# The patch transforms of a convolution block on 64 by 64 tiles of TensorE

## The chip, the cores and the metric

The program runs on one core of a Trainium2 chip. A core has a matrix engine (PE, or TensorE, whose weight loads are a row of their own, PEld), a vector engine (DVE), a scalar engine (ACT), GpSimd (POOL) and SyncE (SP), which here only issues DMAs. The engines run their own instruction streams and meet at semaphores. Matmuls write to PSUM, eight banks of 512 float32 columns on each of 128 partitions; SBUF holds everything else. The metric is the device time of the program in microseconds.

## The reference

Two blocks on an image batch x of 4 by 64 by 64 pixels with 16 channels, all in float32. The first mixes channels in the two-dimensional Fourier domain and ends with a depthwise convolution. The second, whose main loop is changed here, is

```
hidden = layernorm(x) @ w_hidden                     # 16 -> 192
q, k, v = split(conv3x3(hidden, w_qkv), 3)           # 64 channels each
out = irfft2(rfft2(patches(q)) * rfft2(patches(k)))  # 8 by 8 patches
out = v * layernorm(out)                             # over the 64 channels
return out @ w_out + x
```

The product of spectra is a circular convolution of q and k on each patch. A patch has 64 pixels. Its real spectrum is kept as 64 real numbers: 32 "first" ones (real parts) and 32 "second" ones (imaginary parts; the four purely real frequencies are paired up among them).

## The kernel before, in words

The second block runs as a loop of 16 steps `s`. A step handles 1024 pixels, two halves `n = 2s` and `2s + 1` of 512 pixels. What each engine does in a step is written out by hand in a loop over `s` in that engine's block, and the order in that loop is the order of its queue. The pieces, with the names used below (a function is named by what it is called in the code; its index `i` is the step whose data it works on):

- `gather(n)` on DVE and `gather9(n)` on ACT copy the convolution's input windows out of SBUF buffers (`ui`, `ui9`, both in `arena`) into `tile` and `tile9` (L394). `conv(n)` on PE (L1356) multiplies them with the folded weights into banks 0 and 1; `conv_out(n)` on ACT (L773) copies q, k and v of 512 pixels out, into one of four `qkv` buffers. The 64 pixels of a patch lie on 64 partitions, two patches on 128, so a transform contracts over 64 partitions.
- `forward(i)` on PE (L1369), one step later: k's spectrum into banks 4 and 5 (with constant `fk`), then q's into banks 2 and 3 (with `fq`). Each is two matmuls of a 64 by 128 weight tile with 512 columns. The 128 output rows are the spectrum twice over, for q as (first, second, first, second), for k as (first, second, second, first), so that one elementwise product holds all four products that a complex product needs.
- `k_out(i)` on ACT (L780) copies k's 1024 columns to `kh`; `product(i)` on DVE (L1008) multiplies q's 1024 columns in PSUM with it into `pr`.
- `inverse(i)` on PE (L1389): two matmuls of a 128 by 64 weight tile (`inv4`) with 512 columns, into bank 6.
- The layer norm: `o_sum` (L1017) and `o_centre` (L1023) on DVE read bank 6, `o_square` on ACT (L791), `o_variance` on DVE (L1037), `root` on ACT (L761), `o_scale` on DVE (L1042, L1043). In the loop these work on the data of step `s - 2`, whose inverse ended the step before.
- `gate` on POOL (L608 to L610), then `turn(s - 3)` on PE (L1409), four 128 by 128 transposes into bank 7, `turned` on ACT (L767), and for two of four steps `unit(u)` on PE (L1435), which projects 16 image columns, `unit_out` on ACT (L801) and `finish(u)` on DVE (L1055, L447), a transpose and the residual sum. `finish` stands at the end of DVE's steps 6, 7, 10, 11 and 14.

DVE's order in a step is `o_sum`, `o_centre`, `o_variance`, `gather(2s+1)`, `gather(2s+2)`, `o_scale`, `product`, then what is extra in that step. `forward(i)` and `product(i)` are guarded by one buffer each: `product(i)` waits for `inverse(i-1)`, `inverse(i)` for `o_centre(i-1)`.

The input of the second image pair (index `g` = 1, loop steps 8 to 15) is made during the loop. After `bordered(1)` (L889) has written it, `part` on ACT (L655, L658) and `split` on DVE (L882, L884) cut it in three bfloat16 parts; `split(1, 0)` makes two subtractions, one for each image, and `split(1, 1)` two more. SP stores the image (`store_padded`, L484) and its parts (`store_parts`, L490) to DRAM, and loads them back as convolution windows with `load_chunk(g, th, b2)`: three DMAs of `load_taps` (L499) and four of `load_last` (L506, L509), some 1.6 MB. `gather(16)` and `gather9(16)` in step 7 are the first that need a chunk of the second pair, `gather(20)` in step 9 the next.

## Time and profile before

| | us |
|---|---|
| median of 3 runs (220.47 to 221.62) | 220.53 |
| the profiled execution | 220.6 |
| its span, first to last instruction | 218.8 |
| PE busy | 205.2 (94%) |
| DVE busy | 158.2 (72%) |
| ACT busy | 131.7 (60%) |
| POOL busy | 78.2 (36%) |

The granted TensorE clock is 1.00 of full speed over the whole span. PE's busy share is high in every slice of the page except a few; the loop of 16 steps runs from about 89 us to the end.
### The profile page before, as it was taken

The numbers are of one execution on the slowest core, as the hardware profiler recorded it, in microseconds if no ns is written. First come the engines' busy times: TensorE is split into PE (matmuls) and PEld (weight loads), VectorE is DVE, ScalarE is ACT, GpSimd is POOL, SyncE is SP. The second block draws the span as 40 slices with busy tenths as digits, with TensorE's granted clock in tenths as the row PEclk, the third lists the DMA queues.
The fourth block names the chain that finished last, engine by engine and source line by source line (L and its number), as shares of the span: only waits on it lengthen the run. The fifth ranks groups of instructions, "written<-read, shape, count | busy, mean of one in ns | idle before, by whom it ended". The sixth has DMA issues, their size and how long they took to land.

```text
span 218.8 us, 4503 instructions
## 1 busy us (share of the span) xinstructions
PE 205.2 (94%) x1716; PEld 129.9 (59%) x1716; DVE 158.2 (72%) x293; ACT 131.7 (60%) x270; POOL 78.2 (36%) x71
## 2 busy tenths in 40 slices
PE   7979999997999899999969999999999999999993
PEld 3368825674467547867537665757565657665560
DVE  2997524459964991868887876898669886788695
ACT  2647488516384852775756767575756575667471
POOL 1360740002240000000437544753466347544642
PEclk9999999999999999999999999999999999999999
DMA  6950000000000049999998299999990000000002
GB/s 215 305 148 0 12 15 6 23 3 4 0 3 0 0 126 226 227 189 186 197 188 200 76 208 200 184 173 189 184 170 0 24 27 0 1 0 28 0 3 72
DMA packets 26002, 20.86 MB, mean 95 GB/s; under 512 B 5126, under 2 KB 24598, under 8 KB 25878
## 3 DMA queue, kind: packets, MB, share of 16 engines
q1 hardware_dynamic: 25388, 20.01, 46.9%
q10 hardware_dynamic: 592, 0.56, 1.0%
q8 instruction: 14, 0.23, 0.5%
q14 instruction: 8, 0.07, 0.1%
HBM read 16.39 MB, written 4.02 MB: 93 GB/s over the span
## 4 chain that ended last, share of the span: by engine, by line
PE 70%; DVE 16%; ACT 4%; DMA 4%; issue 2%; SPq 2%; DVEq 0%; ACTq 0%
PE psum L1356 26%; PE psum L1369 12%; PE psum L1389 6%; PE psum L1299 4%; PE psum L1173 3%; DMA zp<-padded 3%; PE psum L1409 2%; DVE xc L863 2%; PE psum L1207 2%; ACT arena L707 2%; PE psum L1187 2%; DVE st L859 2%; PE psum L1307 2%; DMA xt<-x 2%; PE psum L1217 2%
## 5 line engine op out<-in xcount | busy, mean ns | idle before, releaser
L1356 PEld LDWEIGHTS psum<-wc,tile 128*128 128x128 f32 (+1 forms) x376 | 50.7, 160 | 25.3 <-issue 16.4
L1356 PE MATMUL psum<-wc,tile 128*128 128x192 f32 (+1 forms) x376 | 59.8, 309 | 2.4 <-ACT x L773 1.9
L608 POOL TENSOR_TENSOR zp<-zp,ln 128x512 f32<-128x512 f32 x14 | 17.9, 1277 | 84.2 <-DVE zp L1043 84.2
L1299 PE MATMUL psum<-arena,wdw 102*128 102x512 f32 x48 | 22.2, 597 | 1.3 <-ACT arena L345 1.3
L1008 DVE TENSOR_TENSOR arena<-psum,arena 128x1024 f32<-128x1024 f32 x15 | 18.3, 1220 | 2.4 <-ACT arena L780 2.4
L791 ACT ACTIVATE zp<-zp 128x512 f32<-128x512 f32 x15 | 9.5, 630 | 16.1 <-DVE zp L1023 16.0
L609 POOL TENSOR_TENSOR zp<-zp,ln 128x512 f32<-128x512 f32 x14 | 18.6, 1325 | 1.1
L773 ACT COPY spec<-psum 128x768 f32<-128x768 f32 x16 | 12.7, 792 | 9.8 <-PE psum L1356 9.8
L641 ACT ACTIVATE sq<-xc 128x512 f32<-128x512 f32 x12 | 7.7, 638 | 15.9 <-DVE xc L863 15.9
L1037 DVE TENSOR_REDUCE stat<-zp 128x8 f32<-128x512 f32 x15 | 10.3, 686 | 9.5 <-ACT zp L791 9.5
L1017 DVE TENSOR_REDUCE stat<-psum 128x8 f32<-128x512 f32 x15 | 10.4, 690 | 8.8 <-PE psum L1389 8.4
L394 DVE COPY tile<-arena 128x256 f32<-128x256 f32 x64 | 15.8, 303 | 1.2 <-DMA zp<-padded 1.0
L1389 PE MATMUL psum<-arena,km 128*64 128x512 f32 x60 | 16.2, 618 | 0.1
L1369 PE MATMUL psum<-spec,km 64*128 64x512 f32 x64 | 15.9, 615 | 0.0
L394 ACT COPY tile<-arena 128x128 f32<-128x128 f32 x60 | 15.8, 317 | 0.0
L780 ACT COPY arena<-psum 128x1024 f32<-128x1024 f32 x15 | 14.9, 994 | 0.3 <-PE psum L1369 0.3
L1299 PEld LDWEIGHTS psum<-arena,wdw 102*128 102x128 f32 x48 | 8.5, 189 | 10.0 <-issue 8.6
L707 ACT ACTIVATE arena<-psum,wt 128x512 f32<-128x512 f32 (+1 forms) x20 | 10.5, 619 | 4.3 <-DVE psum L923 3.3
L597 POOL TENSOR_TENSOR x<-x,wt 128x512 f32<-128x512 f32 x4 | 5.2, 1303 | 18.6 <-DVE zp L875 18.6
L1023 DVE SCALAR_TENSOR_TENSOR zp<-stat,psum 128x512 f32<-128x512 f32 x15 | 10.3, 688 | 1.3
L610 POOL TENSOR_TENSOR zp<-zp,spec 128x512 f32<-128x512 f32 x8 | 11.0, 1376 | 0.6
L1121 PE MATMUL psum<-arena 128*128 128x512 f32 x16 | 9.0, 713 | 1.4 <-POOL arena L560 1.4
(155 smaller groups left out, 364.7 us busy)
## 6 DMA issues: line engine op xcount, KB each, us to landing
arena<-padded SPq DMA_DIRECT2D x12, 393.0 KB, 11.0
arena<-parts SPq DMA_DIRECT2D x12, 196.5 KB, 9.8
arena<-padded SPq DMA_DIRECT2D x6, 262.0 KB, 11.0
arena<-padded SPq DMA_DIRECT2D x8, 195.0 KB, 4.9
wq<-w_qkv SPq DMA_DIRECT2D x1, 1296.0 KB, 11.8
padded<-tr SPq DMA_DIRECT2D x4, 264.0 KB, 2.1
parts<-tr SPq DMA_DIRECT2D x3, 346.5 KB, 3.2
out<-xt SPq DMA_DIRECT2D x8, 128.0 KB, 1.8
```

The source lines that it names most:

```text
L394: o = copy(dst[:, n % 2, 2 * h:2 * h + 2].rearrange("p a (q x y) -> p (a q) x y", q=2, x=8), a)
L608: pool_link(pool.tensor_tensor(y, y, along(0), ALU.mult))
L609: pool_link(pool.tensor_tensor(y, y, along(1), ALU.add))
L610: pool.tensor_tensor(y, y, v_of(i), ALU.mult).then_inc(gated, 1)
L707: act.activation(gl[:, n % 2, b, 0:w], mix_bank(n, b)[:, 0:w], ACT.Gelu, bias=vec("b_fc")).then_inc(gelu1, 1)
L773: act.copy(qkv[n // 2 % 4][:, n % 2].rearrange("p (a t) c -> p a (t c)", a=2), psum[:, 512 * conv_base(n):512 * conv_base(n) + 1024].rearr ...
L780: act.copy(kh, psum[:, 2048:3072]).then_inc(k_ev, 1)
L1008: dve.tensor_tensor(pr, psum[:, 1024:2048], kh, ALU.mult).then_inc(prod, 1)
L1299: last = mm(bank[4 + t4][:, :], wdw[:, dy].rearrange("p x h -> p (x h)"), uw[0:KW, 4 * t4:4 * t4 + 4, 2 * g:2 * g + 2, dy:dy + S], start=( ...
L1356: last = mm(bank[conv_base(n) + a][:, HID * h:HID * h + HID], stationary[:, n % 2, 2 * h + a, :], moving, start=first and h == 0, stop=not ...
L1369: last = mm(bank[2 + 2 * part + q][:, :], const(name)[rows], src, start=True, stop=True)
L1389: last = mm(o_bank(i)[64 * q:64 * q + 64, :], const("inv4"), pr[:, 512 * q:512 * q + 512], start=True, stop=True)
```

## The change

The transforms of steps 0 to 14 are cut to 64 by 64 weight tiles, of which the array holds four (two rows by two columns).

- `forward`: q's spectrum is made once, not twice: four matmuls (two row tiles, two column tiles) of 256 columns each. k's is made in two orders, (first, second) in columns 0 to 255 of a bank and (second, first) in columns 256 to 511: eight matmuls of 256 columns. Twelve in place of four. Column tile `e` holds the half `e` of the 1024 pixels.
- `product` reads q's 256 columns of each bank twice, by a broadcast in its access pattern; it still writes 1024 columns.
- `inverse`: eight matmuls of 256 columns with the constant `inv8`. Row tile `e` writes to its own bank, the upper half of bank 6 or the lower half of bank 7 (`o_all`), and two matmuls sum there.
- `turn` writes to the two outer halves of banks 6 and 7, and `unit` to the upper half of bank 2. For that PE's order changes: `turn` before `conv(2s+1)`, and `unit` at the end of the step before. On ACT `turned` comes before `gather9(2s+2)`, and `unit_out` at the start of the step.
- `gather(7)` returns to its regular place in step 3, and the four subtractions of `split(1, ...)` are spread over DVE's steps 3, 4, 5 and 6, one in each; before they stood as two in step 2, one in step 3 and one in step 4. ACT's second half of `part` moves to steps 4 and 5, and SP stores the fourth image (padded form and parts) only after the load of the third image's first chunk.
- `inverse(0)` waits for all four of `bordered`'s signals (before: three), `inverse(i)` for `turned(i-2)`, `forward(i)` for `unit_out` in steps that have one.

```diff
@@ -125,7 +125,9 @@
     pair = (np.arange(32) >= len(slots))[:, None]
-    put("inv4", np.concatenate([ir, np.where(pair, ii, -ir), np.where(pair, 0, ii), np.where(pair, 0, ii)]))
+    inv4 = np.concatenate([ir, np.where(pair, ii, -ir), np.where(pair, 0, ii), np.where(pair, 0, ii)])
+    put("inv4", inv4)
+    put("inv8", np.tile(np.concatenate([inv4[0:64], inv4[64:128]], 1), (2, 1)))
     put("rep", np.concatenate([np.tile(np.eye(C), (1, WJ)), np.zeros((C, WJ))], 1))
...
@@ -414,8 +416,8 @@
-        def o_bank(i):
-            return bank[6]
+        o_all = psum[:, 3072 + 256:3072 + 768]
+        turn_halves = psum[:, 3072:4096].rearrange("p (a n) -> p a n", a=4)[:, 0:4:3, :]
...
@@ -429,11 +431,11 @@
-        def yt_bank(i):
-            return bank[6 if i == 13 else 7]
+        def turned_of(i):
+            return bank[6].rearrange("p (a n) -> p a n", a=2) if i == 13 else turn_halves
         def unit_bank(u):
-            return bank[7 if u < 5 else (4, 5, 6)[u - 5]]
+            return bank[2][:, 256:512] if u < 5 else bank[(4, 5, 6)[u - 5]]
...
@@ -533,11 +535,11 @@
                 load_chunk(0, 1, b2)
-            for b in (2, 3):
-                store_padded(b)
-                store_parts(b)
             for th in range(2):
                 for b2 in range(2):
+                    if th == 0:
+                        store_padded(2 + b2)
+                        store_parts(2 + b2)
                     sp_.wait_ge(tiled, 8 * th + 4 * b2 + 4)
...
@@ -764,7 +766,7 @@
                     act.wait_ge(pj_mm, unit_after(i - 2 if i % 4 < 2 else i - 4) + 1)
-                act.copy(yt[:, i % 4].rearrange("p e n -> p (e n)"), yt_bank(i)[:, :]).then_inc(yt_ev, 1)
+                act.copy(yt[:, i % 4], turned_of(i)).then_inc(yt_ev, 1)
...
@@ -802,6 +804,9 @@
             for s in range(16):
+                u = unit_after(s - 4)
+                if u is not None and u < 5:
+                    unit_out(u)
                 if s >= 2:
...
@@ -811,21 +816,20 @@
                     k_out(s - 1)
+                if 3 <= s < 15:
+                    turned(s - 3)
                 if s < 15 and s != 1:
                     gather9(2 * s + 2)
-                u = unit_after(s - 4)
-                if u is not None and u < 5:
-                    unit_out(u)
                 conv_out(2 * s + 1)
...
                     gather9(4)
-                if 3 <= s < 15:
-                    turned(s - 3)
                 if s < 15:
                     gather9(2 * s + 3)
-                if s in (1, 2):
-                    for b2 in range(2):
-                        part(1, s - 1, b2)
+                if s == 1:
+                    part(1, 0, 0)
+                    part(1, 0, 1)
+                if s in (4, 5):
+                    part(1, 1, s - 4)
...
@@ -1005,7 +1009,8 @@
                     dve.wait_ge(o_mm, i)
-                dve.tensor_tensor(pr, psum[:, 1024:2048], kh, ALU.mult).then_inc(prod, 1)
+                four = lambda a: a.rearrange("p (q s n) -> p q s n", q=2, s=2)
+                dve.tensor_tensor(four(pr), four(psum[:, 1024:2048])[:, :, 0:1, :].broadcast_to([P, 2, 2, 256]), four(kh), ALU.mult).then_inc(prod, 1)
...
@@ -1014,13 +1019,13 @@
                 dve.wait_ge(o_mm, i + 1)
-                dve.tensor_reduce(out=stat[:, i % 2, 0, :], in_=groups(o_bank(i)), axis=AX.X, op=ALU.add).then_inc(o_summed, 1)
+                dve.tensor_reduce(out=stat[:, i % 2, 0, :], in_=groups(o_all), axis=AX.X, op=ALU.add).then_inc(o_summed, 1)
...
                 dve.wait_ge(o_summed, i + 1)
-                dve.scalar_tensor_tensor(out=groups(oc[:, i % 3]), in0=per_group(stat[:, i % 2, 0, :]), scalar=-1.0 / CH, in1=groups(o_bank(i)),
+                dve.scalar_tensor_tensor(out=groups(oc[:, i % 3]), in0=per_group(stat[:, i % 2, 0, :]), scalar=-1.0 / CH, in1=groups(o_all),
                                          op0=ALU.mult, op1=ALU.add).then_inc(o_centred, 1)
...
@@ -1073,7 +1078,7 @@
                     variance(2, 1)
-                if s >= 1 and s not in (2, 3):
+                if s >= 1 and s != 2:
                     gather(2 * s + 1)
...
@@ -1086,11 +1091,8 @@
                     gather(4)
-                if s == 2:
-                    gather(7)
-                    split(1, 0)
-                if s in (3, 4):
-                    split(1, 1, (s - 3,))
+                if 3 <= s < 7:
+                    split(1, (s - 3) // 2, ((s - 3) % 2,))
                 u = unit_after(s - 4)
...
@@ -1362,11 +1364,16 @@
                     pe.wait_ge(prod, i)
-                for part, name, signal in ((1, "fk", fk_mm), (0, "fq", f_mm)):
-                    for q in range(2):
-                        rows = slice(64 * q, 64 * q + 64)
-                        src = qkv[i % 4][rows, :, :, CH * part:CH * part + CH].rearrange("p e t c -> p (e t) c")
-                        last = mm(bank[2 + 2 * part + q][:, :], const(name)[rows], src, start=True, stop=True)
+                u = unit_after(i - 3)
+                if u is not None and u < 5:
+                    pe.wait_ge(pj_ev, u + 1)
+                for part, name, swaps, signal in ((1, "fk", 2, fk_mm), (0, "fq", 1, f_mm)):
+                    for s in range(swaps):
+                        for e in range(2):
+                            for q in range(2):
+                                rows = slice(64 * q, 64 * q + 64)
+                                last = mm(bank[2 + 2 * part + q][64 * e:64 * e + 64, 256 * s:256 * s + 256], const(name)[rows, 64 * s:64 * s + 64],
+                                          qkv[i % 4][rows, e, :, CH * part:CH * part + CH], start=True, stop=True)
                     last.then_inc(signal, 1)
...
@@ -1382,11 +1389,17 @@
                 if i == 0:
-                    pe.wait_ge(tr_ev, 3)
+                    pe.wait_ge(tr_ev, 4)
                 else:
                     pe.wait_ge(o_centred, i)
-                for q in range(2):
-                    last = mm(o_bank(i)[64 * q:64 * q + 64, :], const("inv4"), pr[:, 512 * q:512 * q + 512], start=True, stop=True)
+                if 2 <= i < 14:
+                    pe.wait_ge(yt_ev, i - 1)
+                for s in range(2):
+                    for q in range(2):
+                        for e in range(2):
+                            rows = slice(64 * e, 64 * e + 64)
+                            last = mm(o_all[64 * q:64 * q + 64, 256 * e:256 * e + 256], const("inv8")[rows, 64 * s:64 * s + 64],
+                                      pr[rows, 512 * q + 256 * s:512 * q + 256 * s + 256], start=(s == 0), stop=(s == 1))
                 last.then_inc(o_mm, 1)
...
@@ -1396,17 +1409,12 @@
             def turn(i):
-                if i == 0:
-                    pe.wait_ge(tr_ev, 4)
-                else:
-                    pe.wait_ge(yt_ev, min(i, 12))
-                    if i == 13:
-                        pe.wait_ge(o_centred, 15)
-                    elif i < 12 and unit_after(i - 1) is not None:
-                        pe.wait_ge(pj_ev, unit_after(i - 1) + 1)
+                pe.wait_ge(o_centred, i + 2 if i < 12 else 15)
                 pe.wait_ge(gated, i + 1)
+                if i == 13:
+                    pe.wait_ge(yt_ev, 13)
                 for t in range(4):
-                    last = pe.transpose(yt_bank(i)[:, P * t:P * t + P], oc[:, i % 3, P * t:P * t + P], const("ident"))
+                    last = pe.transpose(turned_of(i)[:, t // 2, P * (t % 2):P * (t % 2) + P], oc[:, i % 3, P * t:P * t + P], const("ident"))
                 last.then_inc(yt_mm, 1)
...
@@ -1420,6 +1428,7 @@
                 pe.wait_ge(weighted, n)
+                pe.wait_ge(yt_ev, 13)
                 for t in ts:
...
@@ -1450,17 +1459,17 @@
                     forward(s - 1)
-                u = unit_after(s - 4)
-                if u is not None and u < 5:
-                    unit(u)
+                if 3 <= s < 15:
+                    turn(s - 3)
                 if s == 1:
...
                 conv(2 * s + 1)
-                if 3 <= s < 15:
-                    turn(s - 3)
                 if 1 <= s < 15:
                     inverse(s - 1)
+                u = unit_after(s - 3)
+                if u is not None and u < 5:
+                    unit(u)
...
             inverse(14)
```

PE, steps 5 and 6 of the loop (the names are the program's tiles; `spec`, `sq` and `x` are `qkv` buffers, `km` the constants, `zp` the normalised output `oc`). Before:

```order
L1356 MATMUL psum<-wc,tile 128x192 x8
L1369 MATMUL psum<-spec,km 128x512 x4
L1356 MATMUL psum<-wc,tile 128x192 x8
L1409 MATMUL psum<-km,zp 128x128 x4
L1389 MATMUL psum<-arena,km 64x512 x2
L1356 MATMUL psum<-wc,tile 128x192 x8
L1369 MATMUL psum<-spec,km 128x512 x4
L1435 MATMUL psum<-arena,wt 32x256 x4
L1356 MATMUL psum<-wc,tile 128x192 x8
L1409 MATMUL psum<-km,zp 128x128 x4
L1389 MATMUL psum<-arena,km 64x512 x2
```

After:

```order
L1358 MATMUL psum<-wc,tile 128x192 x8
L1375 MATMUL psum<-spec,km 64x256 x12
L1417 MATMUL psum<-km,zp 128x128 x4
L1358 MATMUL psum<-wc,tile 128x192 x8
L1401 MATMUL psum<-arena,km 64x256 x8
L1444 MATMUL psum<-arena,wt 32x256 x4
L1358 MATMUL psum<-wc,tile 128x192 x8
L1375 MATMUL psum<-spec,km 64x256 x12
L1417 MATMUL psum<-km,zp 128x128 x4
L1358 MATMUL psum<-wc,tile 128x192 x8
L1401 MATMUL psum<-arena,km 64x256 x8
```

The transforms have 12 and 8 instructions of 64x256 for 4 and 2 of 512 columns. `turn` (L1409, now L1417) has moved before the second `conv`, and `unit` (L1435, now L1444) from behind `forward` to the end of the step before.

DVE, from the product of step 2 to the end of step 3 (`arena<-psum,arena` is the product; `xc<-tr` and `tr<-xc,tr` are subtractions of `split`; `tile<-arena` is `gather`). Before:

```order
L1008 TENSOR_TENSOR arena<-psum,arena 128x1024
L394 COPY tile<-arena 128x256 x2
L882 TENSOR_TENSOR xc<-tr 128x512 x2
L1017 TENSOR_REDUCE stat<-psum 128x8
L1023 SCALAR_TENSOR_TENSOR zp<-stat,psum 128x512
L1037 TENSOR_REDUCE stat<-zp 128x8
L394 COPY tile<-arena 128x256 x2
L1042 RECIPROCAL stat<-stat 128x8
L1043 TENSOR_TENSOR zp<-zp,stat 128x512
L1008 TENSOR_TENSOR arena<-psum,arena 128x1024
L884 TENSOR_TENSOR tr<-xc,tr 128x8x64
```

After:

```order
L1013 TENSOR_TENSOR arena<-psum,arena 128x1024
L1022 TENSOR_REDUCE stat<-psum 128x8
L1028 SCALAR_TENSOR_TENSOR zp<-stat,psum 128x512
L1042 TENSOR_REDUCE stat<-zp 128x8
L396 COPY tile<-arena 128x256 x4
L1047 RECIPROCAL stat<-stat 128x8
L1048 TENSOR_TENSOR zp<-zp,stat 128x512
L1013 TENSOR_TENSOR arena<-psum,arena 128x1024
L886 TENSOR_TENSOR xc<-tr 128x512
```

Between the product of step 2 and the sum of step 3 nothing is left; the two copies of `gather(7)` stand with those of `gather(8)`, and one subtraction follows the product of step 3. In step 6 one of `split(1, 1)` now stands between product and `finish`.

SP, behind the loads of the first pair (`padded<-tr` is `store_padded`, `parts<-tr` is `store_parts`, `arena<-padded` and `arena<-parts` are a chunk's load). Before:

```order
L484 DMA padded<-tr 128x528
L484 DMA padded<-tr 16x528 x2
L490 DMA parts<-tr 336x1x528
L490 DMA parts<-tr 48x1x528
L484 DMA padded<-tr 128x528
L484 DMA padded<-tr 16x528 x2
L490 DMA parts<-tr 336x1x528
L490 DMA parts<-tr 48x1x528
L499 DMA arena<-padded 48x8x262 x2
L499 DMA arena<-padded 32x8x262
L506 DMA arena<-parts 48x8x262 x2
L509 DMA arena<-parts 16x8x262 x2
```

After:

```order
L486 DMA padded<-tr 128x528
L486 DMA padded<-tr 16x528 x2
L492 DMA parts<-tr 336x1x528
L492 DMA parts<-tr 48x1x528
L501 DMA arena<-padded 48x8x262 x2
L501 DMA arena<-padded 32x8x262
L508 DMA arena<-parts 48x8x262 x2
L511 DMA arena<-parts 16x8x262 x2
L486 DMA padded<-tr 128x528
L486 DMA padded<-tr 16x528 x2
L492 DMA parts<-tr 336x1x528
L492 DMA parts<-tr 48x1x528
```

The first load of the second pair has moved ahead of the stores of the fourth image, whose parts are the last that DVE makes.

## Rows read from the trace of the kernel before

**Rows 1.** The page's chain that ended last, by engine.

```profile
PE 70%; DVE 16%; ACT 4%; DMA 4%; issue 2%; SPq 2%; DVEq 0%; ACTq 0%
```

**Rows 2.** The chain in order of time, steps 7 and 8: start us, us, what.

```profile
143.50 0.57 PE psum L1435 x8
...
149.17 1.92 PE psum L1369 x8
...
152.92 0.44 PE psum L1409 x4
...
153.35 1.01 PE psum L1389 x4
```

**Rows 3.** Timeline of DVE, steps 8 and 9: start us, us, engine line op, tiles, count.

```profile
149.57 0.69 DVE L1037 TENSOR_REDUCE stat<-zp 128x8 f32<-128x512 f32 x1 [0.70 <-ACT zp L791]
...
150.18 0.89 DVE L394 COPY tile<-arena 128x256 f32<-128x256 f32 x4
...
151.82 1.22 DVE L1008 TENSOR_TENSOR arena<-psum,arena 128x1024 f32<-128x1024 f32 x1
...
154.41 0.69 DVE L1017 TENSOR_REDUCE stat<-psum 128x8 f32<-128x512 f32 x1 [1.37 <-PE psum L1389]
...
155.20 0.69 DVE L1023 SCALAR_TENSOR_TENSOR zp<-stat,psum 128x512 f32<-128x512 f32 x1
...
156.59 0.69 DVE L1037 TENSOR_REDUCE stat<-zp 128x8 f32<-128x512 f32 x1 [0.70 <-ACT zp L791]
```

**Rows 4.** Timeline of ACT: the square in step 9.

```profile
155.93 0.63 ACT L791 ACTIVATE zp<-zp 128x512 f32<-128x512 f32 x1 [1.26 <-DVE zp L1023]
```

**Rows 5.** Source view of L1435 in step 7: pass ns min/median/max, first and last start.

```profile
L1435 PE MATMUL psum<-arena,wt x8: 379/391/403, 143.4 to 143.7; 128*32 128x256 f32 x8
```

**Rows 6.** Timeline of PE: the first halved transform at the end, and its follower.

```profile
203.68 1.13 PE L1379 MATMUL psum<-x,km 64*128 64x256 f32 x8
...
204.75 1.08 PE L1389 MATMUL psum<-arena,km 128*64 128x512 f32 x4
```

**Rows 7.** Timeline of PE: first passes of the inverse in steps 1, 2, 3, 14.

```profile
101.24 0.65 PE L1389 MATMUL psum<-arena,km 128*64 128x512 f32 x2
...
107.83 1.08 PE L1389 MATMUL psum<-arena,km 128*64 128x512 f32 x4
...
117.05 1.08 PE L1389 MATMUL psum<-arena,km 128*64 128x512 f32 x4
...
197.10 0.65 PE L1389 MATMUL psum<-arena,km 128*64 128x512 f32 x2
```

**Rows 8.** Timeline of DVE: bordered, split (steps 2, 4), product and finish (step 7).

```profile
100.03 1.53 DVE L889 TENSOR_SCALAR tr<-psum,wt 128x512 f32<-128x512 f32 x2
...
109.45 2.36 DVE L882 TENSOR_TENSOR xc<-tr 128x512 f32<-128x512 f32 x2
...
123.67 0.85 DVE L884 TENSOR_TENSOR tr<-xc,tr 128x512 bf16<-128x512 f32 x1
...
144.23 1.22 DVE L1008 TENSOR_TENSOR arena<-psum,arena 128x1024 f32<-128x1024 f32 x1
...
145.83 1.47 DVE L447 TENSOR_TENSOR xt<-sq,x 128x256 f32<-128x256 f32 x1
```

**Rows 9.** Timeline of SP: the fourth image's parts, then the third's first chunk.

```profile
124.55 1.24 SPq L490 DMA_DIRECT2D parts<-tr  x2
...
125.90 1.67 SPq L499 DMA_DIRECT2D arena<-padded  x3
...
128.88 1.41 SPq L509 DMA_DIRECT2D arena<-parts  x2
```

**Rows 10.** DMA issues in three stretches: from 109.4, 124.5, 128.8 us: us to landing.

```profile
padded<-tr SPq DMA_DIRECT2D x1, 264.0 KB, 8.3
...
parts<-tr SPq DMA_DIRECT2D x1, 346.5 KB, 3.1
...
arena<-parts SPq DMA_DIRECT2D x2, 65.5 KB, 8.0
```

More of the change, by code:

```diff
@@ L55 @@
 MORE, NMORE = columns(("dre", S), ("selre", S), ("selim", S), ("nselim", S), ("ev", 2 * S), ("e2", P), ("ident", P),
-                      ("fq", P), ("fk", P), ("inv4", CH))
+                      ("fq", P), ("fk", P), ("inv4", CH), ("inv8", 2 * CH))
 TAPC, NTAPC = columns(("rep", KW), ("onessel", KW), ("one1", KW))
```

## The prediction

> **What bounds the kernel now.** I read the page's chain first, then the chain in order of time over two steps of the loop, then the timelines of DVE, ACT and PE over one step, to see how much the next engine has left, and last SP's issues with their landings. The page's chain says 70% PE [rows 1]. In order of time, from step 4 on, it is PE alone, without a gap: conv, `forward` 1.92, conv, `turn` 0.44, `inverse` 1.01, and `unit` 0.57 in five of the steps [rows 2]. From the inverse of step 3 to that of step 14 there are 80.05 us [rows 7] for 11 steps, of which 5 have a unit: (80.05 - 5 x 0.57) / 11 = 7.02 us for a plain step.
>
> That invites to count PE's saving once per step. But PE has company. There is a ring through DVE and ACT that a step must go round once, since each inverse reads a product that DVE makes after it has worked on the inverse before. From the timelines [rows 3, 4]: sum 154.41 to centring 155.20, 0.79; to the square 155.93, 0.73; to the variance 156.59, 0.66; then variance 149.57 to product 151.82, 2.25, in which DVE is busy without a gap (variance, four copies, reciprocal, scaling); the product 1.22; then the inverse, 1.08 [rows 7], with 0.05 on each side (its end, 153.35 + 1.01 = 154.36 [rows 2], is 0.05 ahead of the sum at 154.41 [rows 3]; I take the same ahead of it). Together 6.83 us. The slack of the ring is thus 7.02 - 6.83 = 0.19 us a step, and no saving on PE beyond that can be had while DVE's order within a step is kept, and it is kept.
>
> In steps 6, 7, 10, 11 and 14 DVE has `finish` behind the product. The product ends at 144.23 + 1.22 = 145.45 and the residual sum at 145.83 + 1.47 = 147.30 [rows 8], 1.85 later. Without `finish` the next sum could start 0.05 + 1.08 + 0.05 = 1.18 after the product. So such a step takes the ring 6.83 + 0.67 = 7.50 us, against 7.59 on PE (7.02 + 0.57).
>
> **The change, part by part.**
>
> *Forward.* Its eight passes of 512 columns go in four turns, two row tiles at a time, in 1.92 [rows 2]. The halved transform at the end does four turns of 256 columns in 204.75 - 203.68 = 1.07 [rows 6]. So 256 columns cost (1.92 - 1.07) / 4 = 0.21 a turn, and a group 0.22 besides. The new one has 24 passes of 256 columns; four tiles at a time that is six turns, 6 x 0.213 + 0.22 = 1.50, 0.42 less. Bounds: with the four tiles in pairs twelve turns, 2.77, 0.85 more; below six turns nothing can go. That four small tiles do run together here shows `unit`: its eight passes of 379 to 403 ns, in two groups of four, start within 0.3 us [rows 5] and the whole costs 0.57. Those are four column tiles, not two by two; I take six turns.
>
> The Trainium skill, "TensorE: Matmul & The Clock Gate", section "Packing small matmuls", says that a weight load overlaps with matmuls in flight only when the row group differs. By that rule the two column tiles of a row tile would go one after the other. `unit`'s rows are against it, since its four tiles share all rows; by the rule the time would be that of the third rival below.
>
> *Inverse.* Two turns of 512 columns become four of 256: as many columns, 1.01 as before. Bounds: 0.85 more in pairs, and 0.05 less or more for the first turn's latency. `product` reads two separate halves twice over, `o_sum` and `o_centre` read over a bank's border; element counts are the same, so I keep 1.22 and 0.69. No row shows such a pattern; bounds -0.05 to +0.2 a step.
>
> *PE's order.* A plain step of PE comes to 7.02 - 0.42 = 6.60, under the ring's 6.83: PE will wait 0.2 a step, for the product. `turn` ahead of the second conv and `unit` behind the inverse take no time of the ring as long as PE has this slack; `conv_out` now has only the inverse (1.01) between two convs for its 0.8 us, enough if ACT is free, which it is: `turned` has moved ahead of it.
>
> *Start, step 1.* `inverse(0)` now waits for both parts of `bordered`, which end at 100.03 + 1.53 = 101.56 [rows 8], while it started at 101.24 [rows 7]: +0.37 with the signal. The ring carries this on, so the inverse of step 2 comes at 107.83 + 0.37 = 108.20.
>
> *Step 3.* Before, 9.22 us lie between the inverses of steps 2 and 3 [rows 7], since two copies and two subtractions (109.45 to 111.81 [rows 8]) stand ahead of the sum. They leave, and the step is a plain turn of the ring: 6.83, -2.39. One subtraction returns behind the product of steps 3, 4 and 5 each. At 0.85 [rows 8], of which 0.77 are past the product's end, it hides under the 1.18 of the inverse. If it must share with POOL as the pair did (2.36, so up to 1.7 for one), 0.5 comes back in steps 3 and 4.
>
> *Step 6.* Here the fourth subtraction stands with `finish`: nothing hides it, +0.77.
>
> *Step 7, the wait that is new.* `store_parts(2)` needs the third subtraction, and that has moved from step 3 to step 5. Inverses: 108.20, 115.03, 121.86, 128.69 (step 5), 135.52 (step 6). The product of step 5 ends 0.05 ahead, at 128.64, the subtraction at 129.41; SP issues at 129.44. In the trace before the same sequence of store and load began at 124.55, and the chunk's last issues, the pair from 128.88 on, land 8.0 us after issue [rows 9, 10], for the later one (about 129.6) at 137.6: 13.1 us after the store. So the chunk lands at 142.5, or up to 0.6 later because `load_last` must await the parts' landing (3.1 [rows 10], hidden before); I take 142.8. `gather(16)` wants it in step 7: product of step 6 ends 135.47, subtraction +0.77, `finish` +1.85, sum at 138.09, variance 2.18 later at 140.27, third of the four copies 1.0 later [rows 3], at 141.28. A wait of 1.5 us, on DVE, in the ring. Bounds 0.3 to 3 (first loads between 12 and 14.5 us). Inverse of step 7: 142.8 + 1.24 + 1.22 + 0.05 = 145.3. The second chunk: its padded store is queued behind the first chunk and lands just behind it, at about 143.9 (as before, when it took 8.3 behind a load [rows 10]); its load, 11.7 from its first issue to the end (137.6 - 125.90 [rows 9]), lands at 155.7. `gather(20)` wants it 2.51 ahead of the inverse of step 9, 145.3 + 7.50 + 6.83 = 159.6, thus at 157.1: in time by 1.4.
>
> *Sum.* Start +0.37. Step 3 -2.39. Steps 4 to 14: 7 plain of 6.83, 4 with `finish` before them of 7.50, 0.77, and 1.5: 80.08 for 80.05, +0.03. From the inverse of step 14 to the one that follows: 204.75 - 197.10 = 7.65 before [rows 6, 7], PE-bound, one forward less 0.42: 7.23 (the ring with `finish`, and two copies less, is as long). The tail is as it was. 0.37 - 2.39 + 0.03 - 0.42 = -2.4. The profiled execution took 220.6, so 218.2; the median of the runs, 220.53, is the same to 0.1.
>
> **The rivals.**
>
> 1. *The chunk is in time* (store and load are quicker on idle queues, or DVE's steps longer): no wait in step 7, 1.5 less, 216.7. For it: both bounds of the wait are near; against it: the load is bound by its bytes, and its row was taken with an empty queue too.
> 2. *The ring is longer than added up*: the product's broadcast or the two-bank reads cost 0.1 to 0.2 a step, over 13 steps 1.3 to 2.6, or the subtractions share with POOL: 219.5 to 220.8, no change that shows.
> 3. *Two tiles at a time, not four*: forward 0.85 more, inverse 0.85 more, PE 7.02 + 1.70 = 8.72 a step. Over 14 steps +23.8, less 2.2 of step 3's gap: about 242, much slower. Against it [rows 5].
> 4. *Slower by the loads*: the first chunk comes late by over 3 us, and the second, whose stores queue behind the first, by as much again. From 3.5 us of waiting beyond my 1.5 the kernel is slower; at 14.5 us for the first load and 15 for the second it is 218.2 + 1.4 + 2 = 221.6, and 222.5 if the third follows. For it: all loads of the second pair now start 4 us later; against it: 1.4 us of slack at the second and more at each later one, as steps of two gathers (14.3) are longer than a chunk's 9.
> 5. *PE bounds after all* because the ring gives way somewhere: 6.60 a step, 0.23 less in 11, and no wait: about 214.
>
> **How the numbers follow.** Forecast 0.46 (218.2, its own range 217.5 to 219.2), rival 1 0.20, rival 2 0.16, rival 3 0.06, rival 4 0.09, rival 5 0.03. What a measurement here can tell from no change is about 0.5%, 1.1 us: faster is under 219.4, slower over 221.6. Faster: 0.46 + 0.20 + 0.03, and a little of rival 2: 0.72. The same: the rest of rival 2 and some of 4: 0.16. Slower: 0.12. The range 216.4 to 220.9 takes in rivals 1 and 2 and leaves out 3, 5 and most of 4.
>
> **What would show it.** Forward's 24 passes in 1.5 us with starts in fours; a plain step of 6.83 with PE waiting some 0.2 ahead of the inverse for DVE; no gap of PE in step 3; in step 7 DVE waiting for the DMA at a copy, some 1.5 us, and none in step 9. The forecast is wrong if forward takes over 2 us, if the product is over 1.3, if plain steps stay at 7.0, or if copies wait in step 9 too.

## The result, and the profile after

| kernel | median us (runs) | profiled execution, span |
|---|---|---|
| before, run beside after | 221.07 (220.47 to 222.04, 4 runs) | - |
| after | 218.94 (217.6 to 219.5, 4 runs) | 219.09, 217.3 |
| after, measured again | 219.17 (217.94 to 220.14, 6 runs) | 220.1, 218.3 |

The ratio is 0.989, interval 0.984 to 0.994; measured again 0.990, 0.986 to 0.994. So the kernel became faster by 1.1%, 2 us; that is clear of the noise, and less than 2%. One of the eleven executions of before beside the repetition took 403.23 us, is called slow and is left out of the ratio. The forecast was 218.2.

The page's chain is no longer PE's [rows 1]: the ring over DVE and ACT is in it, and a DMA that was not there.

```profile
PE 38%; DVE 34%; DMA 9%; ACT 8%; issue 6%; SPq 3%; DVEq 0%; ACTq 0%
```

One plain step and the start of the next, timeline of PE (start us, us, engine line op, tiles, count, in brackets the idle time ahead and its releaser). It answers to [rows 2, 6].

```profile
153.00 1.09 PE L1401 MATMUL psum<-arena,km 64*64 64x256 f32 x16
154.05 1.87 PE L1358 MATMUL psum<-wc,tile 128*128 128x192 f32 x12
155.85 1.53 PE L1375 MATMUL psum<-spec,km 64*64 64x256 f32 x24
157.31 0.66 PE L1417 MATMUL psum<-km,zp 128*128 128x128 f32 x4
157.80 1.80 PE L1358 MATMUL psum<-wc,tile 128*128 128x192 f32 x12
159.86 0.88 PE L1401 MATMUL psum<-arena,km 64*64 64x256 f32 x12 [0.26 <-DVE arena L1013]
```

`forward` has 24 passes in 1.53 us where eight took 1.92, and ahead of the next inverse PE now waits 0.26 us for the product. From 153.00 to 159.86 the step took 6.86. The source view of `forward` (pass ns min/median/max, first and last start) answers to [rows 5]:

```profile
L1375 PE MATMUL psum<-x,km x24: 376/376/427, 149.3 to 150.5; 64*64 64x256 f32 x24
```

24 passes of 376 ns start within 1.2 us, so several run at a time. In the `forward` of the step shown above the passes start in six groups of four, at 155.85, 156.12, 156.34, 156.55, 156.77 and 156.98, with 0.02 us from the first to the last start in a group. These are the six turns of four tiles.

The same step on DVE has the order and durations of [rows 3]: no price of the new shapes shows.

```profile
154.16 0.69 DVE L1022 TENSOR_REDUCE stat<-psum 128x8 f32<-128x512 f32 x1 [1.41 <-PE psum L1401]
154.96 0.69 DVE L1028 SCALAR_TENSOR_TENSOR zp<-stat,psum 128x512 f32<-128x512 f32 x1
156.34 0.69 DVE L1042 TENSOR_REDUCE stat<-zp 128x8 f32<-128x512 f32 x1 [0.70 <-ACT zp L793]
...
158.59 1.22 DVE L1013 TENSOR_TENSOR arena<-psum,arena 128x1024 f32<-128x1024 f32 x1
```

Step 7 is where time was lost. First SP, answering to [rows 9], then DVE, then PE around it:

```profile
129.33 1.24 SPq L492 DMA_DIRECT2D parts<-tr  x2
131.09 1.92 SPq L501 DMA_DIRECT2D arena<-padded  x3
134.52 0.82 SPq L508 DMA_DIRECT2D arena<-parts  x2
```

```profile
142.29 0.50 DVE L396 COPY tile<-arena 128x256 f32<-128x256 f32 x2 [1.52 <-DMA arena<-parts]
```

```profile
141.06 1.80 PE L1358 MATMUL psum<-wc,tile 128*128 128x192 f32 x12
144.81 1.09 PE L1401 MATMUL psum<-arena,km 64*64 64x256 f32 x16 [1.96 <-DVE arena L1013]
145.84 3.56 PE L1358 MATMUL psum<-wc,tile 128*128 128x192 f32 x12
```

The third subtraction let the store go at 129.33, the chunk landed at 142.29, and DVE waited 1.52 us in the middle of a ring (here and below, the chain of waits over DVE and ACT that leads from one inverse to the next). That was forecast. What follows was not: the conv behind the inverse took 3.56 us, where its neighbours take 1.80 to 1.90. The windows view (length, busy time of PE, PEld, DVE, ACT, POOL, the granted clock, DMA share, GB/s) says why:

```profile
142.00:144.00 2.00, 0.85 (x8) 0.56 (x6) 1.67 (x5) 1.73 (x6) 0.30 (x1) 1.00 0.58 177
144.00:146.00 2.00, 1.19 (x17) 0.68 (x17) 1.97 (x3) 0.10 (x1) 1.92 (x2) 0.96 0.85 172
146.00:148.00 2.00, 2.00 (x7) 2.00 (x8) 1.89 (x3) 0.00 (x0) 1.65 (x2) 0.50 1.11 158
148.00:150.00 2.00, 2.00 (x19) 1.36 (x21) 1.31 (x5) 1.20 (x2) 0.00 (x0) 0.69 1.14 215
```

The granted clock was 0.50, the 1.2 GHz level, for some 3.4 us from 145.84 on; before it fell PE had been idle for 1.96 us, and was then in the inverse of step 7. In this execution the late DMA thus stands ahead of two losses. That the first brings the second is not shown by this: the kernel before has an idle time of the same length in its step 3, and its clock stayed at 1.00 in the profiled execution.

```profile
114.62 1.87 PE L1356 MATMUL psum<-wc,tile 128*128 128x192 f32 x12 [1.95 <-ACT x L773]
```

The time from one inverse's first pass to the next one's (as in [rows 7]) is the table to which all experiments are compared. The last interval ends at the inverse that follows the one of step 14.

| interval, steps | 1-2 | 2-3 | 3-4 | 4-5 | 5-6 | 6-7 | 7-8 | 8-9 | 9-10 | 10-11 | 11-12 | 12-13 | 13-14 | last |
|---|---|---|---|---|---|---|---|---|---|---|---|---|---|---|
| before | 6.60 | 9.22 | 7.02 | 7.02 | 7.59 | 7.59 | 7.02 | 7.02 | 7.59 | 7.59 | 7.02 | 7.02 | 7.59 | 7.65 |
| after | 6.49 | 6.79 | 6.79 | 6.86 | 7.09 | 9.13 | 8.19 | 6.86 | 7.10 | 7.19 | 7.41 | 6.86 | 7.10 | 7.70 |

Before adds up to 103.51 from 101.24 on, after to 101.55 from 101.66 on: 0.42 later at the start, 1.96 won by the end, 1.54 in all; the profiled executions differ by 1.5. Won are 2.43 in step 3 and 2.70 in nine other intervals, by 0.11 to 0.50 each; lost are 1.54 in 6-7, 1.17 in 7-8, 0.39 in 11-12 and 0.05 in the last.

### The profile page after: what moved, and what is told of

Its sections match the earlier page's. It is cut to its first block, busy times and chain, and to the rows that moved or that the text cites. A ratio compares the mean times of both kernels' runs of the same rounds, so it can differ in the third digit from the quotient of the medians.

```text
span 217.3 us, 5352 instructions
## 1 busy us (share of the span) xinstructions
PE 201.2 (93%) x2136; PEld 137.9 (63%) x2136; DVE 155.7 (72%) x293; ACT 133.1 (61%) x270; POOL 78.4 (36%) x71
## 4 chain that ended last, share of the span: by engine, by line
PE 38%; DVE 34%; DMA 9%; ACT 8%; issue 6%; SPq 3%; DVEq 0%; ACTq 0%
PE psum L1358 9%; DVE arena L1013 6%; PE psum L1401 5%; PE psum L1301 4%; PE psum L1175 3%; DVE tile L396 3%; DMA arena<-parts 3%; DVE zp L1028 3%; DVE stat L1022 3%; ACT zp L793 3%; DMA zp<-padded 3%; DVE xt L449 2%; PE psum L1375 2%; DVE xc L867 2%; DMA parts<-tr 2%
## 5 line engine op out<-in xcount | busy, mean ns | idle before, releaser
L1358 PEld LDWEIGHTS psum<-wc,tile 128*128 128x128 f32 (+1 forms) x376 | 52.2, 164 | 10.2 <-issue 7.2
L610 POOL TENSOR_TENSOR zp<-zp,ln 128x512 f32<-128x512 f32 x14 | 17.9, 1277 | 83.0 <-DVE zp L1048 83.0
L1401 PE MATMUL psum<-arena,km 64*64 64x256 f32 x240 | 16.4, 389 | 4.8 <-DVE arena L1013 3.9
L611 POOL TENSOR_TENSOR zp<-zp,ln 128x512 f32<-128x512 f32 x14 | 19.2, 1369 | 1.1
L396 DVE COPY tile<-arena 128x256 f32<-128x256 f32 x64 | 14.7, 286 | 2.7 <-DMA arena<-parts 1.5
L1401 PEld LDWEIGHTS psum<-arena,km 64*64 64x64 f32 x240 | 7.8, 132 | 9.8 <-DVE arena L1013 6.0
L1375 PE MATMUL psum<-spec,km 64*64 64x256 f32 x192 | 12.2, 384 | 0.0
L1123 PE MATMUL psum<-arena 128*128 128x512 f32 x16 | 9.6, 757 | 1.4 <-POOL arena L562 1.4
```

Source lines behind the costliest of these rows:

```text
L396: o = copy(dst[:, n % 2, 2 * h:2 * h + 2].rearrange("p a (q x y) -> p (a q) x y", q=2, x=8), a)
L610: pool_link(pool.tensor_tensor(y, y, along(0), ALU.mult))
L611: pool_link(pool.tensor_tensor(y, y, along(1), ALU.add))
L1358: last = mm(bank[conv_base(n) + a][:, HID * h:HID * h + HID], stationary[:, n % 2, 2 * h + a, :], moving, start=first and h == 0, stop=not ...
L1375: last = mm(bank[2 + 2 * part + q][64 * e:64 * e + 64, 256 * s:256 * s + 256], const(name)[rows, 64 * s:64 * s + 64], qkv[i % 4][rows, e, ...
L1401: last = mm(o_all[64 * q:64 * q + 64, 256 * e:256 * e + 256], const("inv8")[rows, 64 * s:64 * s + 64], pr[rows, 512 * q + 256 * s:512 * q ...
```

## The experiments

In each, "after" is the changed kernel. Before was run beside them, with a median of 220.41 beside e1 to e4, 220.73 beside e5 to e8, and 221.05 beside r1. A code cut shows the lines that matter; `...` and lines of bookkeeping are left out.

**e1: the third image's two subtractions made first.** They stood in steps 3 and 5, the fourth image's in 4 and 6. Here the two that the first chunk needs stand in steps 3 and 4. PE's work is untouched.

```
-            return b + 3 + 2 * (b // 2)
+            return (3, 4, 6, 8)[b]
-                if s in (4, 5):
-                    part(1, 1, s - 4)
+                if s in (3, 5):
+                    part(1, 1, (s - 3) // 2)
-                    split(1, (s - 3) // 2, ((s - 3) % 2,))
+                    split(1, (s - 3) % 2, ((s - 3) // 2,))
```

> The changed kernel with the four subtractions in the order third image, third image, fourth, fourth, so that its parts are stored one step earlier (end of step 4). Theory (the wait in step 7 is the late chunk, and PE's idle time there is what lowered TensorE's clock): DVE's copies don't wait for a DMA in step 7, the inverses of steps 7 and 8 lie 7.5 us apart and not 8.2, the granted clock is 1.00 throughout, and about 1.6 + 0.7 us go: 216.8. Rival (the clock falls for another reason, or the wait only moves to step 9): 217.5 or no change from 219.

Measured: 216.60 (6 runs, 216.33 to 216.98), ratio 0.981, 0.979 to 0.984. The store and the chunk's issues are 7 to 9 us earlier, no engine waits for a DMA in step 7, and the conv behind that inverse takes 1.90 again. SP and then PE:

```profile
122.11 1.24 SPq L492 DMA_DIRECT2D parts<-tr  x2
```

```profile
142.83 1.09 PE L1401 MATMUL psum<-arena,km 64*64 64x256 f32 x16 [0.35 <-DVE arena L1013]
143.86 1.90 PE L1358 MATMUL psum<-wc,tile 128*128 128x192 f32 x12
```

The intervals 6-7 and 7-8 are 7.52 and 7.40, for 9.13 and 8.19, the others are as they were. So the two intervals give 1.61 + 0.79 = 2.40 us. The 1.61 are the wait, the 0.79 stand in the interval in which the clock was low. The medians differ by 2.3, but before was slower beside after than beside e1; through the ratios to before the gain is 1.7 us, or 1.9 by the repetition of after. It need not be 2.40, since not all executions of after had the low clock.

**e2 and e3: each half of the change alone.** e2 has the new transforms with the old schedule of copies, subtractions and stores, e3 the old transforms with the new schedule.

```
e2, against after:
+            for b in (2, 3):
+                store_padded(b)
+                store_parts(b)
...
-                if 3 <= s < 7:
-                    split(1, (s - 3) // 2, ((s - 3) % 2,))
+                if s == 2:
+                    gather(7)
+                    split(1, 0)
+                if s in (3, 4):
+                    split(1, 1, (s - 3,))
e3: the same edit the other way round, on before
```

> The changed kernel's transforms and PE order with the schedule of subtractions, gather(7), parts and stores of the kernel before. Theory (a step is as long as the ring over DVE and ACT, 6.85, or 7.15 to 7.4 with finish): steps 2 to 3 take 9.2 us as before, no wait for a DMA in step 7, plain steps 6.85: about 218.4, so the small tiles alone bring some 2 us. Rival (the tiles bring what PE saves, 0.42 in each of 15 steps): 214.5; rival (they bring nothing, all of the gain was the schedule): 220.5.

> The kernel before, transforms unchanged, with the new schedule of subtractions, gather(7), parts and stores alone. Theory: steps 2 to 3 shrink from 9.2 to 7.0 (PE-bound), then the chunk is late in step 7 by about 1.3 and PE's clock may fall there; PE-bound steps of 7.02 and 7.59 otherwise: 219.3 to 220. Rival (the schedule is what made the changed kernel faster): 218 to 219.

Measured: e2 218.78 (8 runs), 0.992 (0.988 to 0.995); e3 219.41 (10 runs), 0.994 (0.992 to 0.997). Each wins 1 to 2 us alone, 1.9 and 1.3, and both together win 2.2 to 2.4 by their ratios, not the sum of 3.2.

e2 has the gap of step 3 (9.13) and otherwise after's intervals; from the inverse of step 3 to that of step 14 there are 77.82 us for before's 80.05. PE and DVE in e2's step 3:

```profile
113.15 0.66 PE L1418 MATMUL psum<-km,zp 128*128 128x128 f32 x4 [0.88 <-DVE zp L1026]
114.59 1.87 PE L1359 MATMUL psum<-wc,tile 128*128 128x192 f32 x12 [0.78 <-ACT x L775]
117.02 1.09 PE L1402 MATMUL psum<-arena,km 64*64 64x256 f32 x16 [0.56 <-DVE arena L1011]
```

```profile
108.33 3.44 DVE L884 TENSOR_TENSOR xc<-tr 128x512 f32<-128x512 f32 x2
111.69 0.68 DVE L1020 TENSOR_REDUCE stat<-psum 128x8 f32<-128x512 f32 x1
```

Two subtractions ahead of the sum hold the ring for over 3 us, as in [rows 8], whatever PE's transforms cost. e3 has no such gap (7.03), and keeps PE-bound steps of 7.02 and 7.59: the new schedule is worth 2.2 there. It pays 0.72 back in 6-7, which is 8.31 for 7.59, and 0.38 in 7-8, 7.40 for 7.02:

```profile
142.16 0.49 DVE L394 COPY tile<-arena 128x256 f32<-128x256 f32 x2 [1.24 <-DMA arena<-parts]
```

So the late chunk belongs to the schedule, not to the tiles; with PE's longer steps its wait is 1.24 for 1.52. The clock did not fall. Here also lies why the two gains don't add up. The store that the chunk waits for goes at 129.35 in e3 and 129.33 in after, and the inverse of step 7 starts at 144.69 and 144.81. In after the inverse of step 6 was 0.69 earlier (135.69 for 136.38); all of that is gone one inverse later, since the landing of the chunk sets when it comes.

**e4 and e5: DVE's copies in `gather` halved, with after's transforms and with before's.**

```
-            for h in range(2):
+            for h in ((0, 1) if n < 6 or copy == nc.scalar.copy or e == 4 else (1,)):
```

> The changed kernel with one of the two DVE copies left out in every gather from half 6 on (half of each tile stays stale, so the output is not the reference's): 0.4 us less on DVE's ring per step, nothing less on PE. Theory (ring): plain steps fall from 6.85 to PE's 6.6, those with finish to about 7.0 or 7.17: 2.5 to 3 us less, about 216.3. Rival (PE, its mode changes or the bank waits set the step): plain steps stay 6.85 and the time 219.

> The kernel before with one of the two DVE copies left out in every gather from half 6 on (half of each tile stays stale, so the output is not the reference's). Theory: here PE sets the step, so 0.4 us less on DVE buys nothing from step 4 on: inverses stay 7.02 and 7.59 apart, and only steps 1 to 3 may shorten by some tenths: about 220. Rival (DVE's ring sets the step in both kernels): as in the changed kernel, whose plain steps fell from 6.86 to 6.57, some 0.3 less a step: 217.

Measured in one run each: e4 215.56 (before beside it 220.41), e5 220.09 (before beside it 220.73). Plain steps of e4 take 6.53 to 6.57 in place of 6.79 to 6.86, those of e5 7.02 as ever. The timeline of PE in e4, then in e5:

```profile
151.20 1.10 PE L1401 MATMUL psum<-arena,km 64*64 64x256 f32 x16 [0.39 <-DVE arena L1013]
152.22 1.90 PE L1358 MATMUL psum<-wc,tile 128*128 128x192 f32 x12
154.05 1.53 PE L1375 MATMUL psum<-spec,km 64*64 64x256 f32 x24
155.51 0.66 PE L1417 MATMUL psum<-km,zp 128*128 128x128 f32 x4
156.00 1.80 PE L1358 MATMUL psum<-wc,tile 128*128 128x192 f32 x12
157.77 1.09 PE L1401 MATMUL psum<-arena,km 64*64 64x256 f32 x16
```

```profile
152.77 1.08 PE L1389 MATMUL psum<-arena,km 128*64 128x512 f32 x4
...
159.79 1.08 PE L1389 MATMUL psum<-arena,km 128*64 128x512 f32 x4
```

Some 0.4 us less work on DVE does nothing for the steps of before from step 4 on, and shortens every plain step of after, until PE has no idle time left: 157.77 - 151.20 = 6.57, PE's own length of a step. This is the direct evidence that in plain steps the bound moved from PE to the ring. The intervals 5-6, 9-10 and 13-14, in which a `unit` stands and no `finish`, stay at 7.09 to 7.10 in e4 as in after: PE still bounds those. (In e4's step 7 DVE comes to the copy sooner and waits 2.46 us, for a chunk that lands by 141.78; it is counted in the 215.56.)

**e6: all four subtractions one step earlier**, in steps 2 to 5, so that none stands with `finish`.

```
e6, against e1:
-                if s in (3, 5):
-                    part(1, 1, (s - 3) // 2)
+                if s in (2, 4):
+                    part(1, 1, (s - 2) // 2)
-                if 3 <= s < 7:
-                    split(1, (s - 3) % 2, ((s - 3) // 2,))
+                if 2 <= s < 6:
+                    split(1, s % 2, ((s - 2) // 2,))
```

> The first experiment's order of subtractions, all four one step earlier (steps 2 to 5), so that none stands beside finish in step 6. Theory (a subtraction is free under the inverse and costs only beside finish): inverses of steps 6 and 7 lie 7.18 apart, not 7.52, the rest as there: 216.3. My prediction's price for it was 0.77, which would give 215.8. Rival (a subtraction in step 2, where the chain of the start is tight, costs what it saves): 216.6 and above.

Measured: 216.18 (6 runs, 215.98 to 218.3), 0.979 (0.975 to 0.984). The interval 6-7 is 7.19 for e1's 7.52, the only one that changed by over 0.02. So a subtraction beside `finish` costs 0.33, and without `finish` it costs nothing that shows. Why 0.33 is seen on POOL; DVE and POOL in e6's step 6, then POOL in after's:

```profile
135.44 1.27 POOL L611 TENSOR_TENSOR zp<-zp,ln 128x512 f32<-128x512 f32 x1
135.56 1.43 DVE L449 TENSOR_TENSOR xt<-sq,x 128x256 f32<-128x256 f32 x1
```

```profile
135.70 1.61 POOL L611 TENSOR_TENSOR zp<-zp,ln 128x512 f32<-128x512 f32 x1
```

In every step with `finish` of every run here, the residual sum on DVE ends 0.28 us after the end of an operation of POOL's gate that was under way when it began, however long it has then taken. In e6 this one ends at 136.71 and the sum at 136.99. With the subtraction ahead of the sum, POOL's operation is 1.61 long for 1.27, and the sum moves by those 0.33. No run changes the gate itself, so that DVE waits for POOL here is read from the rows and not tested.

**e7: the ring shortened.** In the steps from 7 on in which no `finish` stands, the product comes ahead of the scaling of the gate's image, and `finish`'s transposition goes into DVE's idle time between centring and variance. On ACT, `k_out` comes ahead of `root` in the same steps. The order of subtractions is that of e6.

```
e7, against e6:
+                    if finishing(s):
+                        out_turn(unit_after(s - 4))
                     o_variance(s - 2)
...
-                if s >= 2:
+                if s >= 2 and not product_first(s):
                     o_scale(s - 2)
...
                     product(s - 1)
+                if product_first(s):
+                    o_scale(s - 2)
```

> The one before, with DVE's ring shortened: in steps 8, 9, 12 and 13 the product stands ahead of o_scale and k_out ahead of root; in the steps with finish its transpose stands in DVE's gap between centring and variance. Theory (ring): the plain steps fall from 6.86 to PE's 6.57, those with finish alone from 7.41 to 7.0, the last from 7.70 to 7.3: about 2 us less, 214.2. Rival (gate on POOL, now 0.9 later, makes turn wait, or k_out ahead of root delays finish): 216 or more.

Measured: 214.51 (6 runs, 214.37 to 214.71), 0.970 (0.967 to 0.974). It beats before by 3.0% and, through the ratios to before, after by 1.9 to 2.0%. About half of the latter was there in e6: the edit itself is worth 1.67 us, 216.18 to 214.51. The intervals 7-8 and 11-12, with a `finish` each, fall from 7.41 to 6.53, PE's own length, and the last from 7.70 to 7.38. More than the 0.43 us of the transposition left `finish`: the residual sum starts early enough to end behind the gate's first operation and not its second, and takes 0.54 to 0.58 us for 1.43 to 1.47:

```profile
135.30 0.55 DVE L456 TENSOR_TENSOR xt<-sq,x 128x256 f32<-128x256 f32 x1
```

The plain steps 8-9 and 12-13 did not fall to 6.57, as was expected of them. There, what the rival named came true in part: `turn` waits for the gate on POOL, which gets its input later (PE's timeline, then the waits of that line):

```profile
152.10 1.53 PE L1389 MATMUL psum<-spec,km 64*64 64x256 f32 x24
154.03 0.63 PE L1431 MATMUL psum<-km,zp 128*128 128x128 f32 x4 [0.41 <-POOL zp L619]
```

```profile
  POOL zp L619: 0.8, 2
```

Intervals 8-9 and 9-10 are 6.98 and 7.24, 0.12 and 0.14 longer than in e6, and 12-13 and 13-14 likewise.

**e8: the wait of step 7 filled.** Ahead of the inverse of step 7 PE does four float32 matmuls of 256 columns (eight passes) on other data, so that it is not idle while the chunk is late. Nothing else differs from after.

```
-                pe.wait_ge(prod, i + 1)
+                if i != 6:
+                    pe.wait_ge(prod, i + 1)
+                if i == 6:
+                    keep_warm(4, km, 6, 256)
+                if i == 6:
+                    pe.wait_ge(prod, i + 1)
```

> The changed kernel with four idle matmuls of 256 columns on PE in step 7, ahead of the inverse, in the time in which PE waits for the late chunk. Theory (PE's idle 2 us there are what makes the chip lower TensorE's clock): the wait stays, the granted clock is 1.00, the conv behind it takes 1.83 and not 3.5, the inverses of steps 7 and 8 lie 7.4 apart and not 8.2: about 218.2, with all runs together and not from 217.6 to 219.5. Rival (the clock falls for another reason): it falls as before, 219.

Measured: 218.46 (10 runs, 217.62 to 220.0), 0.988 (0.984 to 0.991). The conv behind the inverse, timeline of PE:

```profile
144.02 1.92 PE L1123 MATMUL psum<-km 128*128 128x256 f32 x8
145.87 1.09 PE L1406 MATMUL psum<-arena,km 64*64 64x256 f32 x16
146.89 1.90 PE L1358 MATMUL psum<-wc,tile 128*128 128x192 f32 x12
```

1.90 for 3.56, and a granted clock of 1.00. The intervals 6-7 and 7-8 are 16.04 together for after's 17.32; of the 1.28, 0.5 are a shorter wait of DVE (1.02), which leaves the 0.79 of the clock. The price: the product ended at 145.60, and the inverse started 0.27 later behind the filling, for 0.05 in after. In the medians the two kernels can't be told apart, so this edit is no gain that is shown, and its executions do not lie closer together, as was expected, but from 217.6 to 220.0. Its profiled execution lost 1.3 in step 3, where the chunk before came late too:

```profile
113.75 0.50 DVE L396 COPY tile<-arena 128x256 f32<-128x256 f32 x2 [1.23 <-DMA arena<-parts]
```

**r1: after again**, to see what of this repeats.

> The changed kernel once more, unchanged, for the granted clock of more of its runs beside those of the kernel with idle matmuls in the wait (10 runs there, clock 0.996 to 1.000, 217.6 to 220.0 us). Theory (PE's idle time in step 7 lowers the clock): most runs show a clock of 0.992 or less and 218.7 to 219.5, the rest about 217.6. Rival (the fall has nothing to do with that wait, since runs of the kernel before and of the tiling alone have it too): the share of runs at 0.992 or less is as small as in the others, about one in three.

Measured: 219.17. Its profile has the low clock in the same place, from 146.77 to 150.18, behind a PE that was busy for 0.13 of the 2 us before 146:

```profile
144.00:146.00 2.00, 0.13 (x4) 0.13 (x8) 2.00 (x3) 1.11 (x3) 1.24 (x1) 1.00 0.38 51
...
148.00:150.00 2.00, 2.00 (x8) 1.82 (x8) 1.20 (x3) 0.63 (x1) 0.79 (x1) 0.50 1.11 203
```

It also has e8's wait in step 3, 1.06 us. Five of the ten runs of after have a mean granted clock of 0.992 or less (three of six in r1, where "most" was expected), none of e8's ten, of e1's six, of e7's six or e3's ten. That speaks for the idle wait as what the fall follows, but it is not settled. One of e6's six has such a mean (218.3 us), though e6's profile shows no wait in step 7; three of e2's eight have one, and 15 of the 42 runs of before that ran beside the experiments. Before and e2 have their idle times in step 3, 1.95 us in one piece and 0.56 to 0.88 in three; where the clock fell in those runs no profile shows. And e4's profile has PE idle for longer at the same place with no fall at all:

```profile
144.09 1.09 PE L1401 MATMUL psum<-arena,km 64*64 64x256 f32 x16 [2.37 <-DVE arena L1013]
145.12 1.90 PE L1358 MATMUL psum<-wc,tile 128*128 128x192 f32 x12
```

## Why the prediction came out right

*The mechanism.* It rested on this: PE's saving counts only down to the ring, 0.19 a step, and not at 0.42. For plain steps the 6.79 to 6.86 (6.83 forecast), PE waiting 0.26, and above all e4 and e5 show it. PE's own length is 6.53 to 6.57 (6.60). `forward` took 1.53 for 1.50, `inverse` 1.09 for 1.08 in the timeline; rival 3 is out. Product and sums kept their 1.22 and 0.69, so that part of rival 2 is out. Its other part, that the subtractions share with POOL, is so by the rows, but the 0.85 of [rows 8] had that in it already. By the Trainium skill, "TensorE: Matmul & The Clock Gate", section "Packing small matmuls", a weight load overlaps with matmuls in flight only when the row group differs. The forecast read this as a rule by which these tiles would run in pairs. 24 passes of 376 ns in 1.53 us, started in fours, go against that.

*Start.* Forecast +0.37, measured +0.42. One execution says little here: e1, with the same code up to there, has +0.05. Over all profiled executions the first inverse starts at 101.29 to 101.67 in the eight with the new wait, and at 100.92 to 101.24 in the three without; the means, 101.48 and 101.10, are 0.38 apart.

*Step 3.* Forecast -2.39, measured -2.43. e2, which lacks this part, has the gap in full.

*Steps 4 to 14.* Forecast +0.03: 80.08 for 80.05. Measured 80.57 (195.51 - 114.94), +0.52. The terms inside it were less exact than their sum:
- Steps with `unit` and without `finish` were counted at 6.83, for `unit` would "take no time of the ring as long as PE has this slack". In these steps it has none: PE's 6.53 + 0.57 is 7.10, which is over the ring, and 7.10 was measured in three intervals, 0.27 more each. PE's saving came through in them whole, 7.59 to 7.10.
- Steps with `finish` come in pairs. They were counted at 7.50 each and took 7.18 and 7.41: into the first of a pair DVE brings the slack that the PE-bound step ahead of it left. e2, which has these steps without the chunk, has 77.82 from step 3 to step 14; my terms make 7 x 6.83 + 4 x 7.50 = 77.81. Right sum, wrong shares, and so luck: in after the seven intervals without `finish` took 0.85 more than forecast, the four with it 1.14 less, the clock's 0.79 left out.
- The subtraction beside `finish`, +0.77, took 0.33 (e6). The forecast added its length to DVE's. But the residual sum behind it ends 0.28 after POOL's operation (e6), and took 1.03 instead of 1.47 in after, which gives 0.44 back. In a step with `finish` the ring runs over POOL too, which the forecast had left out:

```profile
135.36 0.82 DVE L888 TENSOR_TENSOR tr<-xc,tr 128x512 bf16<-128x512 f32 x1
136.09 0.43 DVE L1060 STREAM_TRANSPOSE sq<-sq 128x256 f32<-128x256 f32 x1
136.56 1.03 DVE L449 TENSOR_TENSOR xt<-sq,x 128x256 f32<-128x256 f32 x1
```

- The wait for the chunk: 1.5 forecast, 1.52 measured; the store at 129.33 for 129.44, the copy that waited for the landing at 142.29 for 142.8. The landing was 0.5 early and so was DVE. `gather(20)` did not wait.
- Missing was the clock: 0.79 us in the step behind the wait, in this execution and in r1's, not in e8's or e4's. The forecast took the wait at its own length. What the fall follows is open (r1).

*The last interval.* Here a step failed: forecast 7.23 for 7.65, measured 7.70. I called it PE-bound, with the ring "as long". It is the ring and something behind it: `finish` moves the sum to 1.50 after the inverse, the copies come 2.8 later, and PE's second conv waits for them:

```profile
200.31 1.90 PE L1358 MATMUL psum<-wc,tile 128*128 128x192 f32 x12 [0.43 <-DVE tile L396]
```

Behind them stand conv (1.83) and the halved transform (1.07), in series, so no time that `forward` saves is seen. e7, which takes the transposition from `finish`, gets 0.32 of it.

In sum: forecast 0.37 - 2.39 + 0.03 - 0.42 = -2.4, measured 0.42 - 2.43 + 0.52 + 0.05 - 0.11 (interval 1-2) = -1.5 in the profile and -2 in the medians. The missing 0.9 are the clock (0.8) and the last interval (0.5), less 0.4 on the subtraction. The chunk wanted in step 3 cost r1 and e8 another 1.1 to 1.3 us that the first profile has not; the forecast had no such wait either.

The comparison itself matters as much. Before's profiled execution is one at full clock, after's is not. Split by the mean granted clock, before's runs beside the experiments took 220.5 in the median where it was above 0.992 (27 runs) and 221.9 where it was 0.992 (15); the ten runs of after took 217.95 and 219.3 (five each). Like against like the gain is 2.5 to 2.6 us, for 2.4 forecast. This split was made after the fact and on few runs, so it is an indication and not a measurement.

## What to carry to other kernels

Before crediting a saving on the busiest engine, add up the ring that the next engines need for one step; in that kind of step the difference is all that can be had, and halving a few copies off the "bound" engine (e4, e5) tests it in a run. Do it for each kind of step: those with `unit` gave the whole saving here, those with `finish` had POOL in their ring. When work is spread out to close a gap, follow it to the DMA that depends on it: ordered by whose data is wanted first, the same four subtractions were worth 2.4 us more in the profiles, 1.7 to 1.9 in the ratios (e1). A wait on a DMA in the middle of such a ring costs its whole length, and more where the clock falls behind it.

## What the runs showed of the hardware that was not expected

- The granted clock fell to 0.50 for 3.4 us after PE had been idle for some 2 us, in after, where no wait from step 2 on had been over 0.29, and in r1. It stayed at 1.00 after 1.34 us of idleness in r1's step 3, with three idle times of 0.56 to 0.88 within 4 us (e2), with PE kept busy (e8), and in two profiles after idle times as long: 1.95 us (before) and 2.37 us (e4). What decides between these is open.
- Four 64 by 64 tiles ran at a time: 24 passes of 376 ns, 1.53 us from the first start to the last end, each group of four some 0.215 us behind the one before.
- DVE's operations with two inputs in SBUF, the subtractions and the residual sum, ended at a fixed distance behind the operation that POOL's gate had under way, as if they waited for it. A subtraction of 128x512 took 0.68 us when it began together with POOL's (before, at 109.45), and otherwise ended 0.55 us after POOL's did: 0.79 to 0.86 us when that was near its end, and 1.76 and 1.75 for the pair in e2 (3.44 together). The second of the pair in [rows 8] took 1.76 of the 2.36. The residual sum ended 0.28 us after POOL's operation and took 0.54 to 1.48 us. (One subtraction, in e4's step 6, has another distance: it took 0.68 and ended 0.60 after.)
